# Second attention: maxima and residual into PSUM by TensorE, one of eight rolled products handed to ScalarE and GpSimd

## The reference

```python
x = x + attn_b(layernorm(x))
# x is (16, 256, 128) and is viewed as (N, S, D); 16 heads of hd = 8
q = (x @ Wq.T).reshape(N, S, H, hd).transpose(0, 2, 1, 3)     # likewise k, v
att = jnp.einsum('nqhd,nkhd->nhqk', q, k)
...
```

## Time and profile before

| what | value |
|---|---|
| median of 3 runs | 1031.94 us (1030.3 to 1033.6) |
| the profiled execution: time, span | 1031.32 us, 1029.5 us |
| second attention: first to last pair of `weigh` | begins 688.18 us, last pair begins 913.21 us after the start of the span |
| granted TensorE clock, mean over the span | 0.92 of 2.4 GHz |

### The profile page before, as it was taken

One profiled execution on the slowest core, in us unless ns is written; L12 is line 12 of the kernel. 1 busy time (PEld: TensorE's weight loads), 2 busy tenths in 40 slices (PEclk: granted clock), 3 DMA queues, 4 the chain that ended last, 5 costly groups with the idle time before them and its releaser, 6 DMA issues.

```text
span 1029.5 us, 24309 instructions
## 1 busy us (share of the span) xinstructions
PE 836.7 (81%) x9668; PEld 630.6 (61%) x9668; DVE 696.2 (68%) x1589; ACT 453.2 (44%) x785; POOL 409.3 (40%) x302
## 2 busy tenths in 40 slices
PE   2899999999999999999996865577887777847755
PEld 1677777778777787777775543444454545524534
DVE  4766666666666666666655776458789899877764
ACT  1666666566665655575661422123233223203230
POOL 1444444444444444444442100035756776672000
PEclk9999999999999999999997888678799999977886
DMA  6000000000000000000000000000111111120001
GB/s 248 2 3 1 0 0 0 0 0 0 0 0 0 0 0 0 0 0 0 0 2 1 1 1 1 0 1 11 22 15 16 20 20 14 17 22 9 1 1 82
DMA packets 71585, 13.13 MB, mean 13 GB/s; under 512 B 66432, under 2 KB 70656, under 8 KB 70912
## 3 DMA queue, kind: packets, MB, share of 16 engines
q1 hardware_dynamic: 71552, 12.67, 5.7%
HBM read 8.48 MB, written 4.19 MB: 12 GB/s over the span
## 4 chain that ended last, share of the span: by engine, by line
PE 42%; DVE 26%; issue 15%; ACT 11%; POOL 3%; DMA 1%; DVEq 1%; ACTq 0%; SPq 0%; POOLq 0%
PE PS L513 6%; DVE a_nm L581 6%; PE PS L470 5%; PE PS L686 3%; ACT a_vh L532 3%; DVE b_prod L770 3%; ACT a_ot L543 3%; PE PS L677 2%; DVE stats L349 2%; PE PS L334 2%; DVE f_xs L362 2%; PE PS L679 2%; PE PS L477 2%; POOL b_w L827 2%; PE PS L462 2%
## 5 line engine op out<-in xcount | busy, mean ns | idle before, releaser
L614 POOL TENSOR_TENSOR a_pl<-a_p,a_ph 128x1024 f16<-128x1024 f32 (+1 forms) x128 | 210.1, 1641 | 306.3 <-ACT a_ph L539 306.3
L536 ACT ACTIVATE a_p<-PS 128x1024 f32<-128x1024 f32 (+1 forms) x128 | 103.9, 812 | 200.6 <-PE PS L477 200.6
L581 DVE TENSOR_REDUCE a_nm<-PS 128x4 bf16<-128x512 f32 (+1 forms) x128 | 121.9, 952 | 27.5 <-PE PS L447 27.4
L827 POOL TENSOR_TENSOR b_w<-b_v,b_e 128x2048 f32<-128x2048 f32 x32 | 136.9, 4302 | 0.0
L577 DVE TENSOR_TENSOR a_vl<-PS,a_vh 128x512 f16<-128x512 f32 x64 | 44.3, 692 | 129.9 <-ACT a_vh L532 129.9
L539 ACT ACTIVATE a_ph<-PS 128x1024 f16<-128x1024 f32 (+1 forms) x128 | 103.9, 812 | 0.0
L570 DVE TENSOR_TENSOR a_qk_l<-PS,a_qk_h 128x512 f16<-128x512 f32 x128 | 87.1, 680 | 15.8 <-ACT a_qk_h L529 15.8
L677 PE MATMUL PS<-b_kh,w_rolls 128*128 128x256 f16 x256 | 71.6, 306 | 30.5 <-DVE b_prod L770 29.1
L770 DVE TENSOR_TENSOR b_prod<-PS,b_qt 128x512 f32<-128x512 f32 x128 | 84.1, 677 | 17.4 <-PE PS L679 17.4
L492 PE MATMUL PS<-a_vh,a_ph 128*128 128x65 f16 x768 | 83.8, 195 | 1.3 <-POOL a_pl L614 1.3
L494 PE MATMUL PS<-a_vl,a_ph 128*128 128x64 f16 x768 | 83.9, 194 | 0.0
(11 more groups left out here) (214 smaller groups left out, 2120.3 us busy)
## 6 DMA issues: line engine op xcount, KB each, us to landing
scratch_dram<-b_o SPq DMA_DIRECT2D x32, 64.0 KB, 4.0
b_y<-scratch_dram SPq DMA_DIRECT2D x16, 128.0 KB, 2.1
out_dram<-X SPq DMA_DIRECT2D x2, 1024.0 KB, 3.9
w_rest<-rest_dram SPq DMA_DIRECT2D x1, 1846.0 KB, 15.0
X<-x_dram SPq DMA_DIRECT2D x1, 1792.0 KB, 11.0
w_first<-first_dram SPq DMA_DIRECT2D x1, 1600.0 KB, 6.8
w_rolls<-rolls_dram SPq DMA_DIRECT2D x1, 512.0 KB, 15.4
X<-x_dram SPq DMA_DIRECT2D x1, 256.0 KB, 3.2
```

What stands on the lines that cost most here:

```text
L536: act.activation((a_p0, a_p1)[j][:, me, :, :, :].rearrange("p a h q -> p a (h q)"), TT[:, :, 0:512 - 256 * j], ACT.Exp, scale=EA ** -0.5)
L581: dve.tensor_reduce(a_nm[:, nx, j, :].rearrange("p (a h) -> p a h", a=2)[:, :, 0:2], MM[:, :, 0:256 * (j + 1)].rearrange("p a (h k) -> p a ...
L614: pool.tensor_tensor(*(n[:, g % 2, :, :, :].rearrange("p a h q -> p (a h q)") for n in (pl, p, ph)), ALU.subtract).then_inc(a_split, 1)
L827: pool.tensor_tensor(b_w8[:, j, :, :, :], rolled_values(par, j, 0, H), rolled_exps(par, j, 0, H), ALU.mult).then_inc(b_weighed, 1)
```

## The change

The maxima come out of VectorE negated and in bf16 (`b_nm`), and TensorE adds them to the scores in PSUM with one matmul against the identity (new step `shift`); ScalarE's exponential reads PSUM. The residual goes the same way: TensorE adds `X` through an identity and the bias through two one-row float16 matmuls (`b_bo_h`, `b_bo_l`), and ScalarE copies the sum to `X` (step `add`). The bias halves and a row of ones are made once ahead of the loop. Of the eight rolled products VectorE makes seven; for the last, ScalarE copies the rolled keys from PSUM to `b_kr` in SBUF, and GpSimd multiplies. TensorE's matmuls of roll 0 move ahead of `soft` (step `early`), those of roll 7 ahead of `xt`. In `qk`, ScalarE makes `b_kh` first and `b_qt` only when VectorE has taken `b_kl`. A step keeps one place in the list for all engines, so GpSimd's new product stands behind both of its `weigh` steps.

```diff
 def b_steps(par, former=True, before=True, ahead=True, ahead2=True):
+    put(one, "v", "early")
     put(True, "soft")
     put(two, "norm")
-    put(one, "v", ("roll", 0), ("roll", 1))
+    put(True, "shift")
+    put(one, ("roll", 0), ("roll", 1))
     put(before, "yt")
     put(former, ("gather", 1), "normal")
     put(two, "apply")
     put(True, ("weigh", 0), ("weigh", 1))
...
     put(before, "add")
-    put(one, ("roll", 6), ("flip", 0))
+    put(one, ("roll", 6), ("flip", 0), ("roll", 7))
     put(two, "xt")
-    put(one, ("roll", 7), ("dots", 1))
+    put(one, ("dots", 1))
     put(True, ("gather", 0))
     put(two, "qk")
     put(one, ("flip", 1))
...
+                elif kind == "shift":                      # TensorE
+                    pe.wait_ge(b_maxed, b + 1)
+                    pe.matmul(O[par][:, :].rearrange("p (t s h) -> p t s h", t=QT, s=H), identb[:, :],
+                              b_nm[:, :, :].unsqueeze(2).to_broadcast([128, QT, H, H]), start=False, stop=True,
+                              skip_group_check=True).then_inc(b_shifted, 1)
...
                 elif kind == "dots":
-                    pe.wait_ge(b_multiplied, ROLLS * (b + 1) + 4 * j + 4)
+                    pe.wait_ge(b_multiplied, LAST * (b + 1) + (4, LAST)[j])
+                    if j == 1:
+                        pe.wait_ge(b_pooled, b + 2)
...
                 elif kind == "project":
                     pe.wait_ge(b_turned, b - 1)
+                    for bo in (b_bo_h, b_bo_l):
+                        pe.matmul(dst[:, 0:SEQ].rearrange("p (t d) -> p t d", t=QT), ones_h[:, :],
+                                  bo[:, :].unsqueeze(1).to_broadcast([1, QT, D]), start=bo is b_bo_h, stop=False,
+                                  skip_group_check=True)
                     for t in range(QT):
                         out_t = dst[:, t * 128:(t + 1) * 128]
-                        pe.matmul(out_t, b_yt[:, t * 128:(t + 1) * 128], w["b_wo"][:, :], start=True, stop=False)
-                        ins = pe.matmul(out_t, ones[0:1, :], w["b_bo"][:, :], start=False, stop=True)
+                        pe.matmul(out_t, ident[:, :], X[:, one_tile((b - 2) * QT + t), :].rearrange("p a d -> p (a d)"),
+                                  start=False, stop=False, skip_group_check=True)
+                    for t in range(QT):
+                        out_t = dst[:, t * 128:(t + 1) * 128]
+                        ins = pe.matmul(out_t, b_yt[:, t * 128:(t + 1) * 128], w["b_wo"][:, :], start=False,
+                                        stop=t == QT - 1, skip_group_check=True)
...
                 elif kind == "qk":                         # ScalarE
-                    act.activation(b_qt[:, par, :], src[:, 0:SEQ], ACT.Copy)
                     act.activation(b_kh[:, par, :], src[:, SEQ:2 * SEQ], ACT.Copy).then_inc(b_hi, 1)
+                    act.wait_ge(b_lo, b + 3)
+                    act.activation(b_qt[:, par, :], src[:, 0:SEQ], ACT.Copy).then_inc(b_q, 1)
...
+                elif kind == "roll" and j == LAST:
+                    act.wait_ge(b_rolled, ROLLS * (b + 2))
+                    wait(act, b_pooled, b + 1)
+                    act.activation(b_kr[:, :], T[j % 2][:, :], ACT.Copy).then_inc(b_copied, 1)
...
                 elif kind == "soft":                       # VectorE
                     dve.wait_ge(b_flipped, 2 * (b + 1))
                     sc = O[par][:, :].rearrange("p (t s h) -> p t h s", t=QT, s=H)
-                    link(dve.tensor_reduce(b_m[:, :, :], sc, X_AXIS, ALU.max))
-                    dve.tensor_tensor(b_e[:, par, :, :, :], sc, b_m[:, :, :].unsqueeze(3).to_broadcast([128, QT, H, H]),
-                                      ALU.subtract).then_inc(b_shifted, 1)
+                    dve.tensor_reduce(b_nm[:, :, :], sc, X_AXIS, ALU.max, negate=True).then_inc(b_maxed, 1)
...
+                elif kind == "roll" and j == LAST:         # GpSimd
+                    pool.wait_ge(b_copied, b + 2)
+                    wait(pool, b_dotted, 2 * b + 2)
+                    pool.tensor_tensor(b_prod[:, j, :, :], b_kr[:, :].rearrange("p (e t) -> p e t", e=2),
+                                       b_qt[:, 1 - par, :].unsqueeze(1).to_broadcast([128, 2, SEQ]),
+                                       ALU.mult).then_inc(b_pooled, 1)
```

More of the change, by code:

```diff
@@ L44 @@
 ROLLS = H // 2
+LAST = ROLLS - 1
 class Chain:
@@ L134 @@
 A_EPILOGUE = [("turn", 0, 0), ("pv", 0, 0), ("pv", 0, 1), ("normal", 0, 0), ("turn", 1, 0), ("project", 1, 0)]
-B_PROLOGUE = [("norm", 0, 0), ("apply", 0, 0), ("xt", 0, 0), ("qk", 0, 0), ("v", 1, 0)]
+B_PROLOGUE = [("norm", 0, 0), ("apply", 0, 0), ("xt", 0, 0), ("qk", 0, 0), ("v", 1, 0), ("early", 1, 0)]
 for m in range(ROLLS):
@@ L243, in build @@
         ident, identb = w["ident"], w["identb"]
-        ones = sb("ones", [128, 128])
+        ones, ones_h = sb("ones", [128, 128]), sb("ones_h", [1, 128], F16)
+        b_bo_h, b_bo_l = sb("b_bo_h", [1, D], F16), sb("b_bo_l", [1, D], F16)
         a_wqk_h, a_wqk_l = sb("a_wqk_h", [128, 8, 2, 128], F16), sb("a_wqk_l", [128, 8, 2, 128], F16)
@@ L309, in build @@
         b_kh, b_kl = sb("b_kh", [128, 2, SEQ], F16), sb("b_kl", [128, 2, SEQ], F16)
+        b_kr = sb("b_kr", [128, 2 * SEQ])
         b_prod = sb("b_prod", [128, ROLLS, 2, SEQ])
@@ L670, in do @@
                     ins.then_inc(b_filled, 1)
-                elif kind == "roll":
-                    m = ROLLS * (b + 1) + j
+                elif kind == "shift":
[3 more added lines that the diff above has]
+                              skip_group_check=True).then_inc(b_shifted, 1)
+                elif kind == "early" or kind == "roll" and j > 0:
                     if j == 0:
                         pe.wait_ge(b_lo, b + 2)
-                    wait(pe, b_multiplied, m - 1)
+                    if j == 1:
+                        wait(pe, b_copied, b + 1)
+                    else:
+                        wait(pe, b_multiplied, LAST * (b + 1) + max(j - 1, 0))
                     for e in range(2):
@@ L691, in do @@
                     if j == 0:
-                        wait(pe, b_shifted, b)
+                        wait(pe, b_exped, b)
                     for t in range(QT):
@@ L698, in do @@
                                             ident[:, :].rearrange("p (n h) -> p n h", n=4)[:, :, 0:H],
-                                            start=True, stop=True)
+                                            start=j == 0 and t == 0 and e == 0, stop=False, skip_group_check=True)
                     ins.then_inc(b_flipped, 1)
@@ L715, in b_scalar @@
         def b_scalar(act):
+            bank = [None]
             def do(step, i, fill):
@@ L741, in do @@
                     act.activation(b_st[:, j, :], M[j][:, :], ACT.Copy).then_inc(b_raised, 1)
-                elif kind == "soft":
+                elif kind == "shift":
                     act.wait_ge(b_shifted, b + 1)
-                    act.activation(b_e[:, par, :, :, :], b_e[:, par, :, :, :], ACT.Exp, scale=EB ** -0.5).then_inc(b_exped, 1)
+                    act.activation(b_e[:, par, :, :, :], O[par][:, :].rearrange("p (t s h) -> p t h s", t=QT, s=H),
+                                   ACT.Exp, scale=EB ** -0.5).then_inc(b_exped, 1)
+                elif kind == "project":
+                    bank[0] = R[fill.bank], fill.count
+                elif kind == "add":
+                    projected, count = bank[0]
+                    act.wait_ge(b_filled, count)
+                    act.activation(X[:, bass.ds((b - 2) * QT, QT), :], projected[:, 0:SEQ]
+                                   .rearrange("p (t d) -> p t d", t=QT), ACT.Copy).then_inc(b_added, 1)
                 elif kind == "yt":
@@ L749, in b_vector @@
         def b_vector(dve, chain):
-            link, bank = chain.link, [None]
+            link = chain.link
             def do(step, i, fill):
@@ L755, in do @@
                 if kind in ("ffn_stats", "ffn_apply"):
+                    if kind == "ffn_stats":
+                        dve.wait_ge(b_added, NB // 2)
                     early_norm(dve, link, kind, 1)
@@ L765, in do @@
                                       ALU.subtract).then_inc(b_lo, 1)
-                elif kind == "roll":
+                elif kind == "roll" and j != LAST:
                     dve.wait_ge(b_rolled, ROLLS * (b + 1) + j + 1)
+                    if j == 0:
+                        dve.wait_ge(b_q, b + 2)
                     if j % 4 == 0:
@@ L789, in do @@
                     ins.then_inc((b_gathered, b_summed)[j], 1)
[L790 to L798, removed]
+            run_plan(dve, B_PLAN, do, chain, 2 * 2)
             dve.wait_ge(b_added, NB)
```

11 lines of the change are left out of this document (8 added, 3 removed).

## The result

The changed kernel takes 1113.25 us (median of 4 runs, 1111.83 to 1114.27) against 1032.32 before: a ratio of 1.0785, 95% interval 1.0763 to 1.0806. It is 81 us slower. The forecast was 1110, in a range of 1078 to 1127.

The account below looks back on a forecast made before the run. The prediction took VectorE's queue as the bound before, and a ring through GpSimd's product 7 after. It summed 1031.3 + 48.5 (ring) + 29.5 (clock) + 0.9 (small terms) = 1110 us, range 1078 to 1127.

Parts of the forecast that it names:

- What bounds: Second attention: VectorE's queue sets the period before, 15.0 us a batch; after the change it waits for flip 1.
- The ring: Chain per batch through weigh pair, product 7, dots 1, flip 1, maxima, gather 1: 18.41 us, adding 48.5 in all.
- the full-clock rival of 1081: The ring as forecast, but TensorE's idleness does not slow dots 1 and flip 1: 1081 us, chance 0.17.
- The price of product 7: GpSimd's product behind the weigh pair: 1.15 us from its 128x512 subtraction, ends 0.68 and 2.13.
- The clock: Dots 1, qk and flip 1 at 1.2 GHz after TensorE idles: 2.0 us a batch, 29.5 in all.
- the second rival (1127): Slow clock all the way round the ring, roll 1 included: 1.15 us more for each of fifteen, 1127, chance 0.16.
- The stretch: First to last weigh pair of the second attention: 225.0 us before, plus 48.5 for the ring and 29.5 for the clock.
- Small terms: Prologue 0.6 us, three bias operations ahead of the loop 0.3, epilogue additions 0: 0.9 in the sum.
- VectorE's sum: VectorE's busy sum in the stage falls by about 28 us while the stage grows by 50 or more.
- VectorE's wait: VectorE idle ahead of the maxima, 3 to 5 us in each batch, put down to flip 1's matmuls.
- The rival that the 1.78 us come off: VectorE stays the bound and loses 1.78 us a batch, 28 us in all: 1003 us, chance 0.04.
- The rival of a loss won back: The ring exists, but a misread link of 3 to 4 us falls out: about 1030 us, chance 0.03.

Follow-up runs that it names:

- The experiments with the list: The changed kernel with one step moved in the list, weigh 1 behind GpSimd's product 7 instead of ahead of it: 1038.79 us, 1.0063 of before.
- with the place: The changed kernel, but ScalarE copies and GpSimd makes product 0 ahead of normal, and VectorE makes products 1 to 7: 999.76 us, 0.9678 of before.
- the filled kernel: The changed kernel with 22 matmuls on constants ahead of TensorE's wait for product 7, results overwritten: 1082.01 us, 1.0487 of before.

## Why the prediction was right

- *What bounds.* VectorE bound the kernel before by the busy times of the stretch; the page, with TensorE at 81% and VectorE at 68%, doesn't say so. The runs qualify it: at the full clock the subtraction comes off the period in full, the residual's addition not at all. That VectorE would stop being the bound was read from the order of two rows, the weigh pair's end at 792.10 and the maxima at 791.74. The experiments with the list (1038.8) and with the place (999.8) show that order, not load, is the cause.
- *The ring.* 18.41 us forecast at full clock; with the idle time filled it measures 18.37 to 18.39 in eleven of fifteen periods. This also shows the full-clock rival of 1081 as it would have been: 1082.0.
- *The price of product 7.* 1.15 forecast from the row of 1154 ns, 1.26 measured: 0.11 us low, 1.6 us in all. Dots 1 begins 0.10 or 0.24 us behind its end, by turns, where 0.10 was assumed. That the sum of 18.41 fits the filled kernel so closely is in part luck: there product 7 to dots 1 is 1.31 where the sum has 1.25, and the weigh pair (8.53 for 8.57) and the statistics (1.39 for 1.44) are shorter by as much. The end of 2.13 was far off. The ratio that the Trainium skill gives (GPSIMD Engine Reference, Performance versus the Vector engine) would be 1.33 us: 0.07 high, where the row was 0.11 low. Measured is 1.26 to 0.677, 1.86 times, against its 1.96, with VectorE reading one of its two inputs from PSUM.
- *The clock.* 2.0 us a batch forecast. Dots 1 to the copy 1.99 (forecast 2.00), copy to flip 1 1.13 (0.65 + 0.48 = 1.13), flip 1 to the maxima 1.84 (1.14 + 0.65 = 1.79). Filling the idle time gives back 31 us, 29.5 forecast. The sizes were estimates and partly guesses: flip 1's 0.65 was a choice between 0.4 and 1.0 and came out at 0.70, and the idle time of TensorE was put at 5 us and is 5.9. The clock rises by roll 1, as the forecast had it and the second rival (1127) had not. The Trainium skill's rule (TensorE: Matmul & The Clock Gate, Part 1: The HAM clock gate), that activity releases the slow clock, agrees with these rows. The prediction's own evidence for it was misread, though: its row with 0.50, from 664 to 677, is no idle stretch but has TensorE busy 10.76 of 13 us, and speaks rather for the second rival. An idle stretch at 0.50 in the kernel before is this one:

```profile
660.00:662.00 2.00, 0.00 (x0) 0.00 (x0) 0.76 (x6) 0.00 (x0) 1.01 (x3) 0.50 0.00 0
```

So that the clock would be back by roll 1 was a bet between two rows, and not worked out.

- *The stretch* is 304.95 us, where 225.0 + 48.5 + 29.5 = 303.0 was forecast.
- *Small terms.* 0.9 us were expected and 3.1 measured: 2.0 ahead of the first pair, of which 0.9 already lie ahead of this attention (its first operation on GpSimd starts at 661.83 instead of 660.91), and 1.1 behind the last. These were not followed further.
- *VectorE's sum.* 28 us less was expected, from 0.68, 0.69 and 0.41. The page has 696.2 to 672.2, 24, but it counts time in which two instructions overlap once. Added up by groups of instructions (12.0 of products, 11.1 of subtractions and 6.6 of additions go, against 1.8 of new small ones and small differences), VectorE's work falls from 747.8 to 719.9, the 28 expected.
- *VectorE's wait.* It was to be 3 to 5 us ahead of the maxima, put down to flip 1. It is 6.9 in the period shown: 6.2 for `b_kh` and 0.8 for flip 1. The prediction overlooked that `b_kl` stands ahead of the maxima in VectorE's queue and needs TensorE's qk, behind dots 1. The ring's length does not change by it, as flip 1 still ends last.
- *The rival that the 1.78 us come off.* It needed the ring to be open. Where it is, the time does come off: with GpSimd's product ahead of normal the kernel is 31 us faster than the kernel before in the same series (999.8 to 1030.7), part of it by the clock. The rival of a loss won back, at about 1030, found no link that fell out.

## What to carry to other kernels

Moving work to an idle engine is priced by its place in that engine's queue, not by that engine's load: look at what stands ahead of it there, what waits for it, and whether those two already depend on each other one pass earlier. If they do, add up the links of the ring from start to start and compare that with the present period; here it was 18.4 against 15.0, and with a product moved into GpSimd's idle time ahead of the weigh pair there was no such ring. A chain that leaves TensorE idle must be priced a second time at the lower clock; here that was 31 of 81 us.

## What the runs showed of the hardware that I had not expected

- Work for nothing paid: 22 matmuls of 128x512 float16 in TensorE's idle time in each batch took 31 us off the time (1113.3 to 1082.0).
- Less work on VectorE can win through TensorE's clock rather than through its own time. With 0.41 us a batch moved away, the shortest full period stayed at 14.0 us, but the long ones went from seven to four, the stretch's clock rose from 0.91 to 0.97, and the stretch in the profiled executions fell from 221.0 to 211.5 us.
- GpSimd's 128x2048 product takes 4.28 to 4.32 us wherever a row shows it by itself, and pairs of them 8.5 to 8.6, whether VectorE is 57% or 92% busy beside it; the two did not disturb each other here.
